# Attention, MLP and convolution on one core: all filtered channels of a half turned and projected once, in parts of 128, 128 and 32

## The reference, cut to what matters

```python
HID, OUP = (288, 48)
h = jnp.einsum('oc,bchw->bohw', w1, x)                  # expand 48 -> 288
h = jax.nn.relu(_bn(h, g1, b1, m1, v1))
h = jax.lax.conv_general_dilated(h, wd, window_strides=(1, 1), padding=((1, 1), (1, 1)),
                                 feature_group_count=HID, ...)   # 3x3, each channel by itself
h = jax.nn.relu(_bn(h, gd, bd, md, vd))
h = jnp.einsum('oc,bchw->bohw', w2, h)                  # project 288 -> 48
h = _bn(h, g2, b2, m2, v2)
return x + h
```

## Time and profile before

| what | value |
|---|---|
| median of 3 runs | 1954.59 us (1953.1 to 1954.78) |
| span of the profiled execution | 1952.0 us |
| attention, MLP | until about 1073 us |
| convolution | 1073 to 1952 us, 879 us |
| TensorE busy (share of the span) | 1870.2 us (96%) |
| VectorE, ScalarE, GpSimd busy | 74%, 68%, 33% |
| L1126 expand, matmul | x6144, 322.4 us busy |
| L1145 filter, matmul | x4608, 269.2 us busy |
| L1171 project, matmul | x3072, 195.0 us busy |
| L1180 turn, matmul | x3072, 122.5 us busy |
| L1227 copy on ScalarE | x192, mean 1019 ns |

### The profile page before, as it was taken

The page is one execution under the profiler, slowest core; times in us unless marked ns, Lnnn a source line. Parts: engine busy times, 40 slices in busy tenths (PEclk is TensorE's granted clock), DMA queues, the critical chain, the costliest instruction groups (busy, mean ns, idle before and its releaser), DMA issues.

```text
span 1952.0 us, 74705 instructions
## 1 busy us (share of the span) xinstructions
PE 1870.2 (96%) x29960; PEld 1565.2 (80%) x29960; DVE 1445.8 (74%) x2650; ACT 1322.8 (68%) x2838; POOL 647.1 (33%) x869
## 2 busy tenths in 40 slices
PE   5999999999999996999999999999999999999998
PEld 4888888888888885555555899999999999999997
DVE  5999999999999997666667556566566566566564
ACT  2788878878888885555555666666666666666665
POOL 4333333333333333413100434325334343344240
PEclk9999999999999998999999999999999999999999
DMA  2222222222222222777664444545363454445331
GB/s 67 68 73 76 78 73 76 77 73 76 77 72 77 74 76 77 182 171 179 161 150 111 97 108 126 99 113 126 87 147 86 112 137 102 103 129 105 99 111 34
DMA packets 286410, 198.43 MB, mean 102 GB/s; under 512 B 225991, under 2 KB 275672, under 8 KB 276504
## 3 DMA queue, kind: packets, MB, share of 16 engines
q1 hardware_dynamic: 282114, 189.12, 37.9%
q0 software_dynamic: 2368, 6.25, 1.5%
q10 hardware_dynamic: 1750, 0.39, 0.1%
HBM read 128.36 MB, written 54.72 MB: 94 GB/s over the span
## 4 chain that ended last, share of the span: by engine, by line
PE 56%; ACT 2%; DMA 1%; issue 1%; DVE 0%; SPq 0%; ACTq 0%; DVEq 0%
PE psum L1126 14%; PE psum L1145 13%; PE psum L1171 9%; PE psum L1180 5%; PE psum L680 5%; PE psum L661 3%; PE psum L651 3%; PE psum L666 2%; ACT h2T L1227 1%; DMA room<-tok_mid 1%; ACT h L884 1%; DMA room<-in_ident 0%; ACT room L750 0%; DVE room L885 0%; DVE room L712 0%
## 5 line engine op out<-in xcount | busy, mean ns | idle before, releaser
L934 POOL TENSOR_TENSOR mats<-mats,dscale 112x2048 f32<-112x2048 f32 x72 | 260.8, 3622 | 315.0 <-DMA mats<-in_taps 312.6
L1126 PE MATMUL psum<-ew,xp 64*100 64x96 f32 x6144 | 322.4, 252 | 16.8 <-ACT h L884 13.5
L885 DVE TENSOR_SCALAR h<-psum 100x384 f32<-100x384 f32 x384 | 211.9, 557 | 151.7 <-PE psum L1126 141.6
L1126 PEld LDWEIGHTS psum<-ew,xp 64*100 64x100 f32 x6144 | 295.5, 165 | 26.3 <-ACT h L884 18.6
L1227 ACT ACTIVATE h2T<-psum 96x1024 f32<-96x1024 f32 x192 | 195.6, 1019 | 177.5 <-PE psum L1180 177.5
L1145 PE MATMUL psum<-h,mats 101*64 101x128 f32 x4608 | 269.2, 274 | 1.6 <-issue 0.9
L1145 PEld LDWEIGHTS psum<-h,mats 101*64 101x64 f32 x4608 | 252.0, 137 | 11.8 <-issue 2.0
L884 ACT ACTIVATE room<-psum 64x512 f32<-64x512 f32 (+1 forms) x384 | 206.1, 537 | 78.1 <-PE psum L1145 71.5
L344 PE MATMUL psum<-kb,qa 128*64 128x256 f32 x2048 | 244.0, 380 | 0.8 <-DVE prob L443 0.8
L885 DVE TENSOR_SCALAR room<-psum 64x512 f32<-64x512 f32 (+1 forms) x288 | 174.2, 605 | 64.7 <-PE psum L1145 58.8
L884 ACT ACTIVATE h<-psum 100x384 f32<-100x384 f32 x384 | 186.6, 486 | 48.1 <-PE psum L1126 34.1
(11 more groups left out here) (154 smaller groups left out, 3228.3 us busy)
## 6 DMA issues: line engine op xcount, KB each, us to landing
mats<-in_taps SPq DMA_DIRECT2D x69, 896.0 KB, 5.9
tok_mid<-mid SPq DMA_DIRECT2D x128, 224.0 KB, 1.9
room<-tok_mid SPq DMA_DIRECT2D x64, 448.0 KB, 4.4
piece<-img_mid SPq DMA_DIRECT2D x196, 63.8 KB, 2.4
img_mid<-room SPq DMA_DIRECT2D x128, 97.5 KB, 3.0
kb<-kk SPq DMA_DIRECT2D x512, 24.0 KB
out<-yc SPq DMA_DIRECT2D x32, 384.0 KB, 4.5
scratch<-in_x_tokens SPq DMA_DIRECT2D x126, 96.0 KB, 1.9
```

The lines of the kernel that those rows point to most:

```text
L885: return nc.vector.tensor_scalar(dst, src, 0.0, None, ALU.max)
L934: nc.gpsimd.tensor_tensor(m, m, bc(scale[0:MROWS, at:at + TCH], 2, POUT), ALU.mult).then_inc(mats_scaled, 1)
L1126: mm = nc.tensor.matmul(ring[(j + u) % 4][0:PIN, p:4 * CH:4], xp[hx][rows, 2 * j + p, :], w1[rows, c, :], start=True, stop=True)
```

## The change

The convolution loses its overlap of chunks and handles `h2` once per half.

- `h2` holds all 288 channels of a half: rows of 256, and `h2r` with rows of 32 for the rest. `room` grows from 12288 to 18432 elements.
- Per half TensorE now does expand and filter for chunk 0, 1 and 2, each by itself, and then `close`: 18 items, in two blocks of 9. Items of kind 0 and 1 turn 128 channels of 8 patches of one patch column, for four columns each. Between them stands one item of kind 2, which turns 4 patches x 32 channels at a time for all four columns and is projected by 8 matmuls with 32 rows each.
- A projection is one matmul of 512 columns per `r`. The three kinds add up in one bank per column (`ps_y[col]`, banks 4 to 7), so VectorE adds once per column and block, with `x` and the bias in one instruction.
- `ps_t` is banks 2 and 3 for all turns; turn n waits for copy n - 1.
- Expand waits for the emptying by both engines; the filters wait for all emptying of expand; both engines empty the first unit too. The third chunk expands through banks 4 to 7.
- Patches aren't cut with their borders any more: `xs` holds columns of patches with 130 rows, borders are zero from the start. A piece has 8 rows and two slots per half parity. TensorE waits for all cuts of the next half ahead of the `close`.
- `y` is three buffers of 512 elements; each is stored by two DMAs of 96 KB. SP stores a half before it loads the next taps.

```diff
-        ring = [psum[:, s, :] for s in range(4)]
-        ps_t = psum[:, 4:6, :]
-        ps_y = [psum[:, 6 + s, :] for s in range(2)]
+        ps_t = psum[:, 2:4, :]
+        ps_y = [psum[:, 4 + s, :] for s in range(COLS)]
...
+        KINDS = [*((0, c) for c in range(COLS)), (2, None), *((1, c) for c in range(COLS))]
+        BLOCKS = PR // ROWS
+        ITEMS = [(s, kind, col) for s in range(BLOCKS) for kind, col in KINDS]
...
+        SIDES = [(0, 4), (4, 0), (0, 4)]
+        RINGS = [(0, 4), (0, 4), (4, 4)]
...
+            def expand(h, c, j):
+
+                k, size = CHUNKS * h + c, RINGS[c][1]
+                if j >= size:
+                    n = HALF_E * k + (j - size) // 2 + 1
+                    pe.wait_ge(e_act, n)
+                    pe.wait_ge(e_dve, n)
+                elif j == 0:
+                    evacuated(k - 1, DEPTHS - 1)
...
+            def turn(h, n):
+                s, kind, col = ITEMS[n]
+                if n:
+                    pe.wait_ge(copied, NITEM * h + n)
+                else:
+                    evacuated(CHUNKS * h + CHUNKS - 1, DEPTHS - 1)
+                if kind:
+                    evacuated(CHUNKS * h + CHUNKS - 1, DEPTHS)
+                for a in range(ROWS):
+                    for r in range(2):
+                        rows = slice(ONE * r, ONE * r + ONE)
+                        at = COLS * (ROWS * s + a)
+                        src = (h2r[rows, at:at + COLS, :] if kind == 2 else h2[rows, at + col, P * kind:P * kind + P])
+                        mm = nc.tensor.transpose(ps_t[:, r, POUT * a:POUT * a + POUT], src, ident[rows, rows])
+                mm.then_inc(turned, 1)
+
+            def project(h, n):
+                s, kind, col = ITEMS[n]
+                pe.wait_ge(copied, NITEM * h + n + 1)
...
+                if kind == 2:
+                    for j in range(COLS):
+                        lanes = slice(REST * j, REST * j + REST)
                         for r in range(2):
...
+                            nc.tensor.matmul(ps_y[j][ONE * r:ONE * r + ONE, :], w2[lanes, kind, :], h2T[n % 2][lanes, r, :],
+                                             start=False, stop=False)
+                    return
+                for r in range(2):
+                    mm = nc.tensor.matmul(ps_y[col][ONE * r:ONE * r + ONE, :], w2[:, kind, :], h2T[n % 2][:, r, :],
+                                          start=(kind == 0), stop=(kind == 1))
...
+            def close(h):
+
+                for n in range(NITEM):
+                    turn(h, n)
+                    if n:
+                        project(h, n - 1)
+                project(h, NITEM - 1)
...
+            for h in range(HALVES):
+                pe.wait_ge(cut, PR * (h + 1))
+                if h:
+                    close(h - 1)
+                for c in range(CHUNKS):
+                    for j in range(0, EXPANDS, 2):
+                        expand(h, c, j)
+                    depthwise(h, c)
+            close(HALVES - 1)
...
+            def close(h):
+                for n in range(NITEM):
+                    act.wait_ge(turned, NITEM * h + n + 1)
+                    nc.scalar.activation(h2T[n % 2][:, :, :], ps_t, ACT.Copy).then_inc(copied, 1)
...
+            def add(h, n):
+
+                s, _, col = ITEMS[n]
+                dve.wait_ge(y_ready, NADD * h + COLS * s + col + 1)
+                k = NADD * h + COLS * s + col
+                if k >= YSLOTS:
+                    dve.wait_ge(y_stored[k % YSLOTS], 32 * (k // YSLOTS))
...
+                nc.vector.scalar_tensor_tensor(px(y[k % YSLOTS][:, :]), px(ps_y[col]), c2["b"][:, 0:1], x, ALU.add, ALU.add)\
+                    .then_inc(y_done, 1)
```

More of the change, by code:

```diff
@@ L818, in units_at @@
[L818 to L857, removed]
-        PARTS = [1] * (DEPTHS - 1) + [2]
[L860 to L865, removed]
@@ L882, in relu @@
+        PER_SLOT = PR // SLOTS
         def relu(by_act, dst, src):
@@ L910, in close_borders, with load_piece @@
[L910 to L926, removed]
+        def load_piece(eng, h, j, loaded):
+            b, hx = divmod(h, 2)
+            for r in range(2):
+                x0 = HALF * hx + HALF // 2 * r
+                eng.dma_start(piece[hx][j % SLOTS][ONE * r:ONE * r + C, :, :],
+                              d["img_images"][:, b, PH * j:PH * j + PH, x0:x0 + SIDE]).then_inc(loaded, 16)
@@ L973, in _ @@
             for j in range(PR):
[L974 to L981, removed]
-            close_borders(pool, 0, 0)
-            pool.wait_ge(border_set, 2)
+                if j >= SLOTS:
+                    pool.wait_ge(cut, j - SLOTS + 1)
+                load_piece(pool, 0, j, first_loaded)
+                cut_piece(pool, 0, j)
             pool.wait_ge(w_ready, 4)
@@ L1100, in _ @@
+            for s in range(BLOCKS):
+                store(HALVES - 1, s)
+            for s in range(YSLOTS):
+                sp.wait_ge(y_stored[s], 32 * len(range(s, NADD * HALVES, YSLOTS)))
         @block.tensor
@@ L1237, in _ @@
+            for h in range(HALVES):
+                if h:
+                    close(h - 1)
+                for c in range(CHUNKS):
+                    expanded(CHUNKS * h + c, range(HALF_E))
+                    if c == 0 and h == 0:
+                        for s in range(2):
+                            act.wait_ge(img_stored[s], 32 * (STRIPS // 2))
+                    filtered(CHUNKS * h + c)
+            close(HALVES - 1)
         @block.vector
@@ L1271, in chunk @@
-            def chunk(b, hx, c, last):
-                k = number(b, hx, c)
-                filtered(k)
-                for n in range(NSTEP + 1):
-                    if not last:
-                        expanded(k + 1, units_at(n))
-                    for m in projected_at(n):
-                        add(m, b, hx, c, k)
-            def first():
-                expanded(0, range(0, EXPANDS, 2))
-                for s in range(2):
-                    dve.wait_ge(img_stored[s], 32 * (STRIPS // 2))
@@ new lines, in close @@
+            def close(h):
+                for n in range(NITEM):
+                    if n and n - 1 in FINAL:
+                        add(h, n - 1)
+                add(h, NITEM - 1)
+            for h in range(HALVES):
+                if h:
+                    close(h - 1)
+                for c in range(CHUNKS):
+                    expanded(CHUNKS * h + c, range(HALF_E))
+                    if c == 0 and h == 0:
+                        for s in range(2):
+                            dve.wait_ge(img_stored[s], 32 * (STRIPS // 2))
+                    filtered(CHUNKS * h + c)
```

398 lines of the change are left out of this document (147 added, 251 removed).

## The result

The changed kernel takes 1982.76 us (1978.12 to 1985.34, 4 runs) against 1954.68: it is slower, ratio 1.0143, 95% interval 1.0129 to 1.0158. The forecast was 1969.4, between 1956 and 1986, and slower with a chance of 0.88. So the sign and the range hold, but the loss is 28 us and not 15, and the time lies near the upper end of the range. The profiled execution spans 1982.4 us, 15.6 more than the 1966.8 of the sum. The rest of this document is about what these are made of.

What follows compares the result with a forecast made beforehand. TensorE's work was taken to bound the kernel before. Expand 43.98, filters 32.8 and close 34.4 make 111.2 us per half; eight from 1073.2, plus 4.3, end at 1966.8, +14.8 on the span, giving 1969.4 us, range 1956 to 1986.

Steps and rivals of the forecast that it cites:

- The 5 us less work per half: TensorE's own work per half, with turns and projections each 24 to 18: from 103.4 to 98.2 us.
- terms of the loop: Close: copy 1.02, hand-over 0.06, turn's start to copy's start 0.69; lower bound 1.78 us, 1.83 taken per item.
- an item of 1.95 us: Close: pace if turns grew in proportion to 128 weight columns, 0.51 to 0.68; close 36.4 us, time 1985.
- the rival of 3.8 us: Third kind in the close: row groups take turns, 4 x 0.95 = 3.8 us per item; +41 us, 2010; chance 0.05.
- no cost for the new stride in h2: Filters: writes to rows of 256 and 32 channels in place of 96 taken at no cost.
- a rival with 0.14: Start of each close: clock falls once or twice, 9 or 18 us in all, time 1978 to 1987; chance 0.14.
- The stretch 1054 to 1058: MLP turns in the kernel before: TensorE busy 2.21 of 4 us, clock stayed 1.00; cited against a clock fall.
- The rule of the Trainium skill on transposes: Clock rival: transposes don't count as busy for the clock as matmuls do, so a close, a third turns, might fall.
- it just fits, and I take no cost: Next half's cuts end 22 to 26 us after the second chunk's filters, against 25.8 needed; late-cuts rival +14 us, chance 0.07.
- start-up memsets of POOL lie under the MLP: Start of the kernel: POOL's memsets stay off the path, with the convolution starting at 1073.2 as before.
- closes at 1.72 or less: Rival: close items take 1.72 us or less, so not slower; 1939 at the tail's 1.605; chance 0.10.
- the 1.605 of the tail: Step time in the serial tail of the kernel before, TensorE-bound, turns alternating bank pairs; 17 x 0.225 = 3.8 us less per close.

Runs made afterwards that it cites:

- the run with the filled gap: Changed kernel plus three extra matmuls, results not read, between the first and second turn of every close, where TensorE idled; 1974.91 us, ratio 1.0105 to the kernel before.

## Why the prediction was right or wrong

**Right: the bound and the sum for the steady part.** Expand alone 14.24 and 14.87 (14.28 and 14.85 forecast), filters 10.83 (10.93), an item 1.83 (1.83), a close 34.3 (34.4). A clean half is 14.24 + 2 x 14.87 + 3 x 10.83 + 34.3 = 110.8 against 111.2. The prices came from stretches of the kernel before where nothing stood beside the work, its first chunk and its serial tail, and not from busy time. So the forecast of slower came out for the reason given: with clean halves, a start at 1073.2 and a last close of 38.0 as in the run with the filled gap, the span is by estimate 1073.2 + 8 x 110.8 + 3.7 = 1963.3 us, 11 more than before, without any of the disturbances. The 5 us less work per half that the prediction counted in slots isn't in the busy time, which fell by 7 us in the whole convolution (it counts a turn to its end, 0.71, where the slot is 0.64, and six closes ran partly at half clock); the sum didn't use it. The prediction's terms of the loop, 1.02, 0.06 and 0.69, add up to 1.77 and not 1.78; the 0.05 for a wider weight load was a guess, and from a turn's start to the copy's start it is now 0.75 (1160.33 to 1161.08).

**Luck: that the time is in the range.** The upper end, 1986, comes from an item of 1.95 us, and items take 1.83. What carried the time from 1969 to 1983 were terms that the sum had at nothing: the start (6.5 us), the clock (7) and the cuts (3.8), less some 4 us by which the sum was too high.

**Right: the third kind.** 1.11 us for 16 instructions; the rival of 3.8 us is refuted.

**Right: no cost for the new stride in h2.** With rows of 256 and 32 channels an emptying takes ScalarE 590 ns and VectorE 694, as before.

**Wrong in size: the clock, held for a rival with 0.14.** The clock fell in six of eight closes, where I had given it one chance in seven. The step that failed is the weight given to the earlier trace rows. The stretch 1054 to 1058 with 2.21 of 4 us busy kept its clock, and I let it speak for the close, though the tail had the same place and order of events as the close (filters end, turn, idle). The price of 1 to 2 us per fall was right: 0.8 to 1.7, about 7 us in all. What happens at the start of a close decides, as the run with the filled gap shows, and not the share of turns all through it: with two bank pairs turns are 0.64 of 1.64 us of an item and the clock stays at 1.00 in all closes of two runs. The rule of the Trainium skill on transposes, cited for that rival, isn't needed for the falls, since in the run with earlier cuts three came in the middle of expand with no turn near; that turns count for less at the start of a close isn't excluded, as no run has turns in the gap in place of matmuls.

**Wrong: "it just fits, and I take no cost".** I had cuts end between 22 and 26 us against a need of 25.8 and priced this at nothing, with 0.07 for 2 us each. Measured: 0.2 to 2.1 us in the halves concerned, 3.8 us in all. With such a margin the term was the mean of what lies above it, not zero. Nor did I ask whether the wait was needed where it stood; moved, it costs nothing.

**Wrong: "start-up memsets of POOL lie under the MLP".** They lie beside it, but VectorE's scaling took 3.39 us in place of 0.65 beside them, at a point where TensorE waits for VectorE. It cost 3 to 5 us of the late start. I costed a moved instruction by its own engine alone.

**Wrong in weight: "closes at 1.72 or less".** The loop isn't faster by itself (0.10 was too much). But the 1.605 of the tail named the remedy: with two bank pairs the item is 1.64, and the time 1945.7 where 1939 was worked out for it.

## What to carry to other kernels

When overlap is given up for fewer instructions, price each part from a stretch where it already runs alone, and then look for a free bank pair or a next stage's matmuls to put into the gap: here each item of a close left TensorE idle beside its copy, and one edit that put matmuls there turned a loss of 1.4% into a gain of 1.1% (1.6% with the memset and the last close mended too). Don't price a margin smaller than its spread at zero, and put a wait at the first use of its data. A memset on GpSimd was not free for VectorE here, nor for what waits for VectorE. And before a late input is blamed for a long group, look where in it the engine stood: the long third expands had their idle time in the middle, not before the filter that needs the taps.

## What the runs showed of the hardware

Eight tiles of 32 rows x 64 columns, float32, work side by side: 16 matmul instructions of 512 columns take 1.11 us, 4 instructions on two tiles 1.08. A gap of 1.5 us between two turns, behind dense work, was followed by a fall of the granted clock to its lower level in six of eight places (five, five and two of eight in three other runs), and by none in eight once three matmuls stood in it. Idle times of 1.5, 2.1 and 2.7 us in the middle of dense matmuls were each followed by a fall too, those of 0.9 and 1.0 us by none. A fall cost 0.8 to 1.7 us. VectorE's 0.65 us of scaling (SBUF to SBUF) took 3.39 and 4.97 us beside a GpSimd memset, and its instructions that read PSUM took no longer.
